# Attention and ternary feed-forward block on one core: all window masks ride in the scores' second pass, a copied query tile, epsilon added on GpSimd, new slots

## The reference, cut to what matters

```python
# x: 4 batches x 2048 tokens x 256, float32; 16 heads of 16; window of 64 keys
x = x + attn(layernorm(x))      # softmax(q k^T / 4 + bias) v, then Wo
x = x + ffn(layernorm(x))       # relu(y Wq1^T + b1) Wq2^T + b2, Wq1 and Wq2 ternary
allowed = (j <= i) & (j > i - 64)          # bias: 0 where allowed, -inf elsewhere
def _layernorm(x, eps=1e-5): return (x - mean(x)) / sqrt(var(x) + eps)
```

## Time and profile before

| | us |
|---|---|
| median of 3 runs (671.62 to 673.49) | 672.49 |
| the profiled execution, its own time | 674.08 |
| its span from first to last instruction | 672.3 |
| PE busy | 645.8 |
| DVE busy | 610.4 |
| ACT busy | 564.0 |
| POOL busy | 562.0 |

### The profile page before, as it was taken

The page is one execution under the profiler, slowest core; times in us unless marked ns, Lnnn a source line. Parts: engine busy times, 40 slices in busy tenths (PEclk is TensorE's granted clock), DMA queues, the critical chain, the costliest instruction groups (busy, mean ns, idle before and its releaser), DMA issues.

```text
span 672.3 us, 23905 instructions
## 1 busy us (share of the span) xinstructions
PE 645.8 (96%) x8049; PEld 556.4 (83%) x8049; DVE 610.4 (91%) x1388; ACT 564.0 (84%) x2483; POOL 562.0 (84%) x837
## 2 busy tenths in 40 slices
PE   7677999999999999999999999999999999998997
PEld 5465778889888888988888898888888898887886
DVE  8889799998999999998999999899999989898974
ACT  6787889888989989888998988899898989788722
POOL 8888899888889888888988888888988888798821
...
GB/s 313 104 120 73 113 87 105 98 106 123 73 130 88 134 100 117 106 96 118 83 133 97 131 106 94 127 77 119 98 135 100 65 136 67 103 87 98 37 48 32
DMA packets 187009, 70.19 MB, mean 104 GB/s; under 512 B 155268, under 2 KB 178438, under 8 KB 186888
## 3 DMA queue, kind: packets, MB, share of 16 engines
...
## 4 chain that ended last, share of the span: by engine, by line
PE 84%; DVE 7%; SPq 2%; ACT 2%; issue 2%; DMA 1%; ACTq 1%; DVEq 0%
PE ps L1239 16%; PE ps L1227 15%; PE ps L1134 12%; PE ps L1112 11%; PE ps L1173 11%; PE ps L1200 6%; PE ps L1186 5%; PE ps L1212 2%; PE ps L1104 2%; PE ps L1160 2%; DVE negm L827 2%; ACT p L626 1%; PE ps L1234 1%; SPq L353 1%; DVE pt L844 1%
## 5 line engine op out<-in xcount | busy, mean ns | idle before, releaser
L626 ACT ACTIVATE p<-ps,negm 128x96 f32<-128x96 f32 x1024 | 335.3, 356 | 13.6 <-DVE negm L827 12.8
L503 POOL TENSOR_TENSOR tl<-pt,th 128x384 f16<-128x384 f32 x256 | 235.0, 918 | 20.7
L626 ACT ACTIVATION_READ_ACCUMULATOR p<-ps,negm 128x1 f32 x1024 | 229.2, 224 | 0.0
L827 DVE TENSOR_REDUCE negm<-ps 128x4 f32<-128x384 f32 x256 | 137.8, 538 | 31.3 <-PE ps L1112 28.3
L501 POOL CAST th<-pt 128x384 f16<-128x384 f32 x256 | 128.8, 503 | 28.1 <-DVE pt L844 27.6
L844 DVE STREAM_TRANSPOSE pt<-p 128x384 f32<-128x384 f32 x256 | 143.6, 561 | 2.4 <-ACT p L626 2.2
L1112 PE MATMUL ps<-k,qbd 128*128 128x96 f16 x1536 | 124.8, 207 | 0.0
L1112 PEld LDWEIGHTS ps<-k,qbd 128*128 128x128 f16 x1536 | 112.4, 113 | 9.7 <-issue 0.3
L1134 PE MATMUL ps<-th,vb 128*128 128x96 f16 (+1 forms) x1120 | 99.5, 204 | 1.6 <-DVE osum L904 1.6
L1134 PE MATMUL ps<-tl,vb 128*128 128x96 f16 (+1 forms) x1120 | 99.5, 204 | 0.0
L1227 PE MATMUL ps<-xTCh,w1T 128*128 128x256 f16 x512 | 97.6, 272 | 0.0
...
## 6 DMA issues: line engine op xcount, KB each, us to landing
...
qbd<-qs SPq DMA_DIRECT2D x252, 32.0 KB, 2.5
vb<-vd SPq DMA_DIRECT2D x248, 32.0 KB, 2.0
x<-in_L_attn_hidden ACTq DMA_DIRECT2D x15, 512.0 KB, 4.0
...
```

The lines of the kernel that those rows point to most:

```text
L503: e.tensor_tensor(tl[g % 2][:, o], pt[n % 3][:, :], th[g % 2][:, o], ALU.subtract).then_inc(s_lo, 1)
L626: ins = e.activation(p[:, 96 * u:96 * u + 96], bank[:, 96 * u:96 * u + 96], ACT.Exp, bias=m[:, u:u + 1], accum_out=r[:, u:u + 1])
L827: e.tensor_reduce(negm[n % 4][:, :], sbank[n % 3][:, 0:384].rearrange("p (a b) -> p a b", b=96), AX.X, ALU.max, negate=True).then_inc(s_mx, 1)
```

## The change

- In all chunks but the first, the second pass of all four groups goes with the mask patterns: `qm` becomes two tiles, `kw` four. The ninth matmul (line 1104) stays in chunk 0 only; the full mask of `first` stays.
- `place_q` writes high and low parts to `qbd[t]` only, on two semaphores. A new DMA, `copy_q`, waits for the high parts and copies the even rows of `qbd[t]` (64 rows of 8 KB, 512 KB) to `qm[t]`; `scores` waits for it. Before, four DMAs of 32 KB wrote `qm`, for t = 0 alone.
- `place_k` issues two DMAs for each of the four groups; before, the groups of t = 1 had one each.
- POOL writes the mask patterns of the additional tiles during the first chunk (`Q_MASK`, `K_MASK`).
- The six small reduces a chunk go from DVE. POOL adds epsilon, and for A also negates the mean. C's norm subtracts the mean and multiplies by rstd, without a shift; `mvC` is doubled.
- Slots: V of a chunk in slots 6 and 9 (10 and 13 before), K of t = 1 in 13 (14), `wo1` in 10 (11), the second `y` in 10 and 11 (9 and 10), statistics of A in slot 6 (8), the multiplication by the inverse in 7 and 15 (6 and 14). PE's slots 12 to 14 then hold: 12: scores, values, t0; 13: scores, K of t = 1; 14: scores, f00. SP's order is K, Q, copy and V in slots 7, 9, 11, 12, and for t = 1 K, Q, copy in slots 16, 17, 17.

```diff
-V_LATE = 9
-A_T, A_K, A_Q, A_V = (1, 2), (5, 14), (6, 15), (10, 13)
-A_STATS, A_RSTD, A_NORM = (-24, -14), -12, (-7, -6)
-N_STATS, N_RSTD, N_NORM = ((-20, 1, 11), (-13, 2, 15)), (-15, 6, 19), ((-11, 7, 23), (-11, 9, 21))
-Q_DMA, K_DMA, V_DMA, A_CARRY = (8, 20), (15, 22), 18, 1
-C_WO, C_STATS, C_RSTD = (8, 11), (10, 14), (12, 16)
-C_T, C_F, C_Y = (12, 17), (14, 20), (18, 25)
+V_LATE = (8, 11)
+A_T, A_K, A_Q, A_V = (1, 2), (5, 13), (6, 15), (6, 9)
+A_STATS, A_RSTD, A_NORM = (-26, -14), -12, (-6, -5)
+N_STATS, N_RSTD, N_NORM = ((-20, 1, 11), (-13, 2, 15)), (-15, 5, 19), ((-13, 8, 22), (-12, 6, 23))
+F_V = (6, 9)
+Q_DMA, Q_COPY, K_DMA, V_DMA, A_CARRY = (9, 17), (11, 17), (7, 16), 12, 1
+C_WO, C_STATS, C_RSTD = (8, 10), (10, 14), (12, 16)
+C_T, C_F, C_Y = (12, 17), (14, 20), (18, 26)
 E_WO, E_T = (C_WO[0], C_T[0]), (C_T[0], C_Y[0])
-OUT_DMA, X_DMA = (24, 31), 37
-X_LATE = (7, 16, 24)
+OUT_DMA, X_DMA = (26, 33), 35
...
-R_INV, R_PARK, R_WIDEN, R_MUL = 9, 10, 11, 14
+R_INV, R_PARK, R_WIDEN, R_MUL = 9, 10, 12, 15
...
-W_WO, K_MASK = (-6, -2), (7, 12)
-V_CLEAR = (8, 15, 19, 22, 26)
+W_WO, K_MASK, Q_MASK = (-7, -2), (5, 8, 11, 15), (-1, 11)
+V_CLEAR = (10, 15, 19, 21, 26)
...
-    return c if t else 1 if n == V_LATE else None if c == 1 else c
+    return 0 if n == F_V[t] - 16 else c if c and c > 1 else 1 if n == V_LATE[t] else None
...
-        mvA = sb("mvA", [128, 4, 3], f32)
-        mvC = sb("mvC", [128, 2, 3], f32)
+        mvA = sb("mvA", [128, 4, 2], f32)
+        mvC = [sb(f"mvC{i}", [128, 2, 2], f32) for i in range(2)]
...
-        qm = sb("qm", [128, 2, 4, 128, 4], f16)
-        ks = [sb(f"k{g}", [128, 1 + g // 2, 64 + CH], f16) for g in range(4)]
-        kw = [sb(f"kw{g}", [128, 16, 96], f16) for g in range(2)]
+        qm = [sb(f"qm{t}", [128, 2, 4, 128, 4], f16) for t in range(2)]
+        ks = [sb(f"k{g}", [128, 64 + CH], f16) for g in range(4)]
+        kw = [sb(f"kw{g}", [128, 16, 96], f16) for g in range(4)]
...
-                if c == 1 and t == 0:
+                if c == 1:
...
+                e.dma_start(ks[g][:, :], bass.AP(tensor=src, offset=row, ap=[[2 * w, 64], [0, 2], [1, w]])).then_inc(d_k[g], 16)
+                if c:
+                    e.dma_start(bass.AP(tensor=kw[g][:, :, :].tensor, offset=0, ap=[[2 * 1536, 64], [1, 1536]]),
+                                bass.AP(tensor=src, offset=row + w, ap=[[2 * w, 64], [32, 16], [1, 96]])).then_inc(d_k[g], 16)
...
-        def place_q(e, c, t, parts=(0, 1, 2)):
+
+
+        def place_q(e, c, t, parts=(0, 1)):
...
-            for i in parts:
-                to, v = ((qbd[t], 0), (qm, 0), (qbd[t], 1))[i]
-                if to is qm and (t == 1 or c == 0):
-                    continue
-                if to is qm and c == 1:
-                    e.wait_ge(s_zm, 1)
...
+            for v in parts:
...
+                                qst[t][32 * h:32 * h + 32, v, :]).then_inc((d_q, d_ql)[v][t], 16)
+
+
+        def copy_q(e, c, t):
+            e.wait_ge(d_q[t], 64 * (c + 1))
+            if c == 1:
+                e.wait_ge(s_zm, t + 1)
+            to, src = (z[t][:, :, :, :, :].tensor for z in (qm, qbd))
+            e.dma_start(bass.AP(tensor=to, offset=0, ap=[[2 * 4096, 64], [1, 4096]]),
+                        bass.AP(tensor=src, offset=0, ap=[[2 * 4096, 64], [1, 4096]])).then_inc(d_qm[t], 16)
...
+                    c = stage_a(n, Q_COPY[t])
+                    if c is not None and c >= 1:
+                        copy_q(e, c, t)
...
-            def mask_queries():
+            def mask_queries(t):
                 e.wait_ge(d_s, 16)
-                e.tensor_copy(qm[:, :, :, :, :].rearrange("p g a j b -> p (g a) (j b)").bitcast(f32),
-                              pr[0][:, 0:256].unsqueeze(1).to_broadcast([128, 8, 256])).then_inc(s_zm, 1)
+                e.tensor_copy(qm[t][:, :, :, :, :].rearrange("p g a j b -> p (g a) (j b)").bitcast(f32),
+                              smask.bitcast(f32).unsqueeze(1).to_broadcast([128, 8, 256])).then_inc(s_zm, 1)
...
-                e.wait_ge(s_mvA, c + 1)
+                e.wait_ge(s_agA, c + 1)
                 if c >= 2:
                     e.wait_ge(s_xnA, 2 * c - 2)
+                e.tensor_scalar(meanA[:, :], mvA[:, :, 0], -1.0, None, ALU.mult)
+                e.tensor_scalar(veA[:, :], mvA[:, :, 1], 1e-5, None, ALU.add).then_inc(s_veA, 1)
+                e.wait_ge(s_veA, c + 1)
...
-                e.wait_ge(s_mvC, h + 1)
+                e.wait_ge(s_agC, h + 1)
                 if h >= 2:
                     e.wait_ge(s_xnC, h - 1)
+                e.tensor_scalar(veC[:, :], mvC[m][:, :, 1], 1e-5, None, ALU.add).then_inc(s_veC, 1)
+                e.wait_ge(s_veC, h + 1)
                 e.tensor_tensor(rstdC[m][:, :], veC[:, :], mhalf[:, 0:2], ALU.pow).then_inc(s_powC, 1)
-                e.wait_ge(s_powC, h + 1)
-                e.tensor_tensor(shiftC[m][:, :], meanC[:, :], rstdC[m][:, :], ALU.mult).then_inc(s_rsC, 1)
...
-                e.wait_ge(s_rsC, h + 1)
+                e.wait_ge(s_powC, h + 1)
                 if h >= 1:
                     e.wait_ge(s_c, USE[(h - 1) // 2, f"t{(h - 1) % 2}"] + 1)
                 for t in range(2):
-                    ins = e.tensor_scalar(xnC[:, t, 0:D - 1], xs[c % NX][:, 2 * u + t, 0:D - 1], rstdC[u][:, t:t + 1],
-                                          shiftC[u][:, t:t + 1], ALU.mult, ALU.add)
+                    ins = e.tensor_scalar(xnC[:, t, 0:D - 1], xs[c % NX][:, 2 * u + t, 0:D - 1], mvC[u][:, t, 0:1],
+                                          rstdC[u][:, t:t + 1], ALU.subtract, ALU.mult)
...
-                    mask_queries()
+                if n in Q_MASK:
+                    mask_queries(Q_MASK.index(n))
...
-                    ins = e.bn_aggr(mvA[:, t, 0:2], stA[:, t, :])
+                    ins = e.bn_aggr(mvA[:, t, :], stA[:, t, :])
                 ins.then_inc(s_agA, 1)
-                e.wait_ge(s_agA, c + 1)
-                e.tensor_reduce(meanA[:, :], mvA[:, :, 0:1], AX.X, ALU.max, negate=True)
-                e.tensor_reduce(veA[:, :], mvA[:, :, 1:3], AX.X, ALU.add).then_inc(s_mvA, 1)
...
-                if h >= 1:
-                    e.wait_ge(s_rsC, h)
+                if h >= 2:
+                    e.wait_ge(s_xnC, h - 1)
                 for t in range(2):
-                    ins = e.bn_aggr(mvC[:, t, 0:2], stC[:, t, :])
+                    ins = e.bn_aggr(mvC[u][:, t, :], stC[:, t, :])
                 ins.then_inc(s_agC, 1)
-                e.wait_ge(s_agC, h + 1)
-                e.tensor_reduce(meanC[:, :], mvC[:, :, 0:1], AX.X, ALU.max, negate=True)
-                e.tensor_reduce(veC[:, :], mvC[:, :, 1:3], AX.X, ALU.add).then_inc(s_mvC, 1)
...
-                e.wait_ge(d_q[g // 2], queries_placed(c, g // 2))
-                e.wait_ge(d_k[g], 16 * NKD[g // 2] * (c + 1))
+                e.wait_ge(d_q[g // 2], 64 * (c + 1))
+                e.wait_ge(d_ql[g // 2], 64 * (c + 1))
+                if c:
+                    e.wait_ge(d_qm[g // 2], 16 * c)
+                e.wait_ge(d_k[g], 32 * (c + 1))
                 if first:
                     e.matmul(bank[:, 0:384], identb[:, :], maskf[:, :], start=True, stop=False, skip_group_check=True)
-                elif g >= 2 or c == 0:
+                elif c == 0:
                     ends = bank[:, 0:384].rearrange("p (u j k) -> p u j k", j=3, k=32)[:, :, 0:3:2, :]
                     seen = maskf[:, 288:384].rearrange("p (j k) -> p j k", k=32)[:, 0:3:2, :]
                     e.matmul(ends, identb[:, :], seen.unsqueeze(1).to_broadcast([128, 4, 2, 32]), start=True, stop=False,
                 for u in range(4):
                     blk = 4 * iq + u
                     for m in range(2):
-                        to = qm if g < 2 and m and c else qbd[g // 2]
-                        keys = (ks[g][:, m, 32 * blk:32 * blk + 96] if g >= 2 or not m else kw[g][:, blk, :] if c
+                        to = qm[g // 2] if m and c else qbd[g // 2]
+                        keys = (ks[g][:, 32 * blk:32 * blk + 96] if not m else kw[g][:, blk, :] if c
                                 else first_kl[g][:, 32 * blk:32 * blk + 96])
                         ins = e.matmul(bank[:, 96 * u:96 * u + 96], to[:, g % 2, blk % 4, :, blk // 4], keys,
-                                       start=(g < 2 and c > 0 and not first and m == 0 and u == 0),
+                                       start=(c > 0 and not first and m == 0 and u == 0),
```

More of the change, by code:

```diff
@@ L131, in _turns @@
     late = {("C", NCH - 1, "wo1"): E_WO[1] + 0.5, ("C", NCH - 1, "t1"): E_T[1] - 0.5}
-    order = [(V_LATE if (stage, c, name) == ("A", 1, 4) else 16 * (c + (1 if stage == "C" else -1)) + late.get((stage, c, name), p), stage == "A", i, stage, c, name)
+    order = [(V_LATE[name - 4] if (stage, c) == ("A", 1) and name in (4, 5) else F_V[name - 4] - 16 if (stage, c) == ("A", 0) and name in (4, 5) else 16 * (c + (1 if stage == "C" else -1)) + late.get((stage, c, name), p), stage == "A", i, stage, c, name)
```

(6 more changed lines are left out.)

46 lines of the change are left out of this document (14 added, 32 removed).

## The result

The changed kernel takes 716.7 us, median of 4 runs (715.91 to 717.57), against 672.56 for the kernel before in the same session: a ratio of 1.0657, 95% interval 1.0635 to 1.0678. It is 44 us slower. The prediction was 663.2, range 657 to 670, with a chance of 0.06 for slower. The profiled execution took 715.9, its span is 714.1, 41.8 more than the span before.

A forecast was written before the change was run, and what follows sets the result against it. PE alone was taken to bound the kernel from 92 to 580 us. Terms -12.0 + 2.1 + 1.4 - 1.8 + 1.0 = -9.3 us took the median 672.5 to 663.2, own range 660.5 to 666 (40%), outer 657 to 670.

The forecast's parts named there:

- POOL gains two instructions for A and swaps shift for add in C ... +0.4 us a chunk: POOL's load: small instructions at 0.195 us each, 0.4 us more a chunk and one semaphore step.
- the cover is there: POOL's waits for the variance, 15.8 us in 11 times, 1.4 a chunk, were to absorb its added work; otherwise 7.5 us.
- 2.4 - 0.9 - 1.5: Room at t1: 2.4 us before, less 0.9 of shorter chunk and 1.5 of later statistics carried by POOL, leaving nothing.
- the masks' 12.0 us: PE's list: 114 mask matmuls removed at 0.109 us each, 12.4 us, taken as a 12.0 us saving.
- It stays covered by PE if its late moments fit: DVE loses 0.6 us a chunk, stays at 94% load, and was to remain hidden behind PE.
- the chain of 2.69 in 2.67 us at t0 to f00: First tight place: ACT's chain to xTCl against PE's work from t0 to f00; wait taken as 0.15 us a chunk.
- the two tight places: t0 to f00, waiting for xTCl, +2.1 us; t1, waiting for xnC, 0.1 us in each of 14 chunks, +1.4 us.
- -1.8 at the end: Chunk 15: the 2.02 us wait for keys goes, ACT's exponentials are next late, so 1.8 us come back.
- +1.0 at the start: First chunk: POOL's additional query and key tiles, 4.8 us of work, taken as +1.0 us, from -1 to +4.
- the 0.4 kept back for chunk 1: Chunk 1: only half of its eight masks counted, since PE waits there anyway; 12.0 taken of 12.4 us.
- the fifth: Rival: new bank or drain waits between A and C take the masks' saving back, 670.5 to 674.5 us; chance 4%.
- The second: Rival: POOL's in-order list becomes the bound, chunk 38.3 us or more, 0.45 to 0.7 lost each, 667 to 670; chance 15%.

The follow-up runs named there:

- e14: The changed kernel with C's norm as add and mult of a mean negated by POOL ahead of the power: 682.2 us, ratio 1.0121.
- e6: e4 with POOL's shift taken out, C's norm being add and mult of the negated mean, made by DVE and doubled: 674.9 us, ratio 1.0037.
- e10: e4 with the first y products in slot 3 instead of 2, plus the edits of e6 and e8: 683.8 us, ratio 1.0170.
- e11: e10 with A's two reduces also made on POOL as small additions: 685.5 us, ratio 1.0197.
- e1: The changed kernel with C's norm back to mult and add, POOL making the negated mean and a shift: 690.7 us, ratio 1.0271.
- e4: The changed kernel with DVE's six reduces, POOL's shift and C's norm as before; masks, copy and slots stay changed: 675.8 us, ratio 1.0052.
- e8: e4 with only the multiplication by the inverse put back to slots 6 and 14, its widening copies to 3 and 11: 675.05 us, ratio 1.0043.

## Why the prediction was wrong

**The step that failed first: "POOL gains two instructions for A and swaps shift for add in C ... +0.4 us a chunk".** This prices the additions, and leaves the norm, which the change turns from mult and add into subtract and mult, at its old 573 ns without saying so. It was an edit costed at nothing with no row for its form. It measured 1253 ns, 2.7 us of POOL a chunk, and 34.5 us of time (716.7 to e14's 682.2). At t1, where I had taken 0.1 us a chunk, PE waited 2.6 in the changed kernel by the distances, and 0.18 in e6, without the slow form and the additions.

**Second, the cover taken for POOL.** "POOL waits 15.8 us in 11 times for just this variance ...; the cover is there": these waits are A's, in slot 3, and for A the cover was indeed there (e10 to e11, the same chunk). C's additions stand elsewhere, behind the split of slot 15 and ahead of t1, where my own count of the room (2.4 - 0.9 - 1.5) had left nothing. From e14 to e6, which differ in where the mean's sign and epsilon are made, are 7.3 us. The sign for C, 0.24 us a half, is the quick form's and not the change's, and no run has epsilon alone on POOL, so that what the change's own additions cost stays open. By the other path, e1 to e4 with the shift kept, 14.9. I read the difference as all of it lying in one row of POOL, so that the order of removal counts; only the sum of a path is firm, 41.8 us either way.

The Trainium skill, GPSIMD Engine Reference, section Engine selection, spoke against such work on GpSimd. The trace agrees in kind: 0.22 to 0.24 us an addition, against 0.15 on VectorE. The factor of two that the Trainium skill gives there, from which the prediction worked out 0.6 us, is for two inputs, while these additions have one. The addition cost more by its place than by its length.

**Third, the masks' 12.0 us.** "It stays covered by PE if its late moments fit": they did not. I compared DVE's load with the whole chunk, 94% before and after. But K of t = 1 left slot 14 and V's half left slot 13, for slots 13 and 9: between slot 13 and slot 2 PE lost 1.3 us of V and two masks, 1.5 in all, DVE lost one drain of 0.68. There DVE's row, which had been as long as PE's before, now sets the time. I followed the chain of 2.69 in 2.67 us at t0 to f00 and stopped at its end; it goes on through some twenty more instructions of DVE to hTl and y. This could have been read in the trace of the kernel before (372.56 and 372.62, above). With form and additions out of the way the kernel (e6) is 2.4 us slower than before, with 12.4 us of matmuls fewer: 14.8 us of waits net, where I had 2.1 + 1.4 at the two tight places, -1.8 at the end and +1.0 at the start, 2.7 in all, or 3.1 with the 0.4 kept back for chunk 1.

Of the rivals, the fifth, "the masks go, but new bank or drain waits between A and C take it back, 670.5 to 674.5", describes e4 and e6 in kind (675.8 and 674.9, just above its range), and got 4%. The second, POOL as the bound, describes the changed kernel in kind, but with 0.45 to 0.7 us a chunk where 3.2 came (41.1 for 37.87).

**What held.** 114 matmuls went. The wait for keys in chunk 15 is gone; next late there is not ACT, as I had it, but oTl for wo, 1.7 us, which comes with the multiplication in slot 15 (0.46 in e8, by the distances). The copy landed in 4.3 us (4.0 taken), and PE never waits for it. xTCl is late for f00 by 0.09 a chunk (0.15 taken). The start with POOL's additional tiles cost nothing: in e4 chunk 2 starts at 95.7 us, before at 96.2 (+1.0 taken). So the 4.4 us lost there in the changed kernel come with the norm and the additions.
